# Four key stacks instead of three in a one-core cross-attention kernel

## What is computed

```python
q = (query @ Wq.T + bq).reshape(B, Sq, H, Hd).transpose(0, 2, 1, 3)      # H = 16 heads of Hd = 16
k = (key @ Wk.T + bk).reshape(B, Skv, H, Hd).transpose(0, 2, 1, 3)       # Skv = 375
v = (value @ Wv.T + bv).reshape(B, Skv, H, Hd).transpose(0, 2, 1, 3)
scores = jnp.einsum('bhqd,bhkd->bhqk', q * SCALE, k)
attn = jax.nn.softmax(scores, axis=-1)
out = jnp.einsum('bhqk,bhkd->bhqd', attn, v)
```

## Time and profile before

| | us |
|---|---|
| median of 3 executions | 563.15 (563.07 to 571.28) |
| the profiled execution, its own time | 567.81 |
| its span, first to last instruction | 566.1 |
| TensorE busy (68% of the span) | 384.2 |
| VectorE busy (68%) | 386.0 |
| ScalarE busy (47%) | 264.0 |
| GpSimd busy (16%) | 88.6 |

### The profile page before, as it was taken

The page is one execution under the profiler, slowest core; times in us unless marked ns, Lnnn a source line. Parts: engine busy times, 40 slices in busy tenths (PEclk is TensorE's granted clock), DMA queues, the critical chain, the costliest instruction groups (busy, mean ns, idle before and its releaser), DMA issues.

```text
span 566.1 us, 9319 instructions
## 1 busy us (share of the span) xinstructions
PE 384.2 (68%) x3004; PEld 256.1 (45%) x3004; DVE 386.0 (68%) x1614; ACT 264.0 (47%) x672; POOL 88.6 (16%) x274
## 2 busy tenths in 40 slices
PE   2899789912339699886898778898999701803006
PEld 2558576601127455563576566676545300203003
DVE  7644999989983768897776666672354477185773
ACT  3853534622221566345465555777453353243440
POOL 6793000000006064540240000000000000000000
PEclk9998699955557899889779998999999955855556
DMA  9800002368202598441675875500894000000002
GB/s 279 234 1 2 0 2 96 123 131 155 68 1 81 117 127 150 141 112 30 113 146 84 164 150 83 84 2 2 326 392 136 0 1 1 1 1 2 1 0 65
DMA packets 38533, 50.95 MB, mean 90 GB/s; under 512 B 5957, under 2 KB 35030, under 8 KB 37334
## 3 DMA queue, kind: packets, MB, share of 16 engines
q1 hardware_dynamic: 38486, 50.37, 37.3%
HBM read 40.28 MB, written 9.97 MB: 89 GB/s over the span
## 4 chain that ended last, share of the span: by engine, by line
PE 40%; DVE 34%; ACT 11%; issue 5%; DMA 5%; POOL 4%; SPq 1%; DVEq 0%; POOLq 0%; ACTq 0%
PE ps L2202 8%; DMA ks<-key_parts 5%; DVE PR L1080 5%; ACT below L1794 4%; PE ps L2036 4%; PE ps L2141 3%; PE ps L2166 3%; PE ps L2152 3%; DVE R L1014 2%; PE ps L1981 2%; DVE below L1417 2%; DVE prod L1076 2%; PE ps L1897 2%; PE ps L2326 2%; DVE PR L1078 2%
## 5 line engine op out<-in xcount | busy, mean ns | idle before, releaser
L1294 DVE TENSOR_REDUCE negm<-ps 112x1 f32<-112x375 f32 x128 | 64.1, 542 | 31.0 <-PE ps L2141 30.6
L1762 ACT ACTIVATE E<-ps 125x448 f32<-125x448 f32 x96 | 49.2, 546 | 30.0 <-PE ps L2152 28.3
L2141 PE MATMUL ps<-ks,qs 96*112 96x375 bf16 x128 | 45.0, 365 | 10.9 <-DMA ks<-key_parts 7.4
L2152 PE MATMUL ps<-qs,ks 99*125 99x112 bf16 x384 | 39.8, 230 | 5.2 <-ACT E L1762 3.4
L2152 PEld LDWEIGHTS ps<-qs,ks 99*125 99x125 bf16 x384 | 35.6, 145 | 13.2 <-ACT E L1762 9.8
L1282 DVE TENSOR_REDUCE acts<-gel 128x4 f32<-128x448 f32 x32 | 19.8, 620 | 30.9 <-ACT gel L1726 30.9
L2293 PE MATMUL ps<-cnt,same 128*128 128x7 bf16 (+1 forms) x22 | 3.6, 166 | 47.1 <-ACT below L1794 43.6
L2166 PE MATMUL ps<-E,v 125*32 125x112 f32 x768 | 32.3, 279 | 0.1
L811 POOL CAST kp<-kx 128x750 bf16<-128x750 f32 x8 | 6.5, 814 | 160.8 <-ACT path L1640 122.3
L1726 ACT ACTIVATE gel<-ps 128x448 f32<-128x448 f32 x32 | 17.3, 544 | 29.3 <-PE ps L2202 29.3
L1080 DVE TENSOR_TENSOR_SCAN PR<-UU,PR,prod 128x94 bf16<-128x94 bf16 x63 | 26.1, 414 | 2.2
(11 more groups left out here) (378 smaller groups left out, 1020.1 us busy)
## 6 DMA issues: line engine op xcount, KB each, us to landing
ks<-key_parts SPq DMA_DIRECT2D x48, 187.5 KB, 6.8
piwT<-fn_process_input_weights SPq DMA_DIRECT2D x4, 2048.0 KB, 16.6
key_parts<-kp SPq DMA_DIRECT2D x48, 93.8 KB
ctx_again<-in_ctx SPq DMA_DIRECT2D x7, 512.0 KB
keys<-kx SPq DMA_DIRECT2D x16, 187.5 KB, 2.2
kx<-keys SPq DMA_DIRECT2D x8, 375.0 KB, 5.9
ctxP<-in_ctx SPq DMA_DIRECT2D x8, 256.0 KB, 6.0
patT<-in_L_ffn_input_patterns SPq DMA_DIRECT2D x1, 2048.0 KB, 17.3
```

What stands on the lines that cost most here:

```text
L1294: drain(dve.tensor_reduce(negm[:, n:n + 1], bank(nm)[0:S, 0:SC], AX.X, ALU.max, negate=True), nm)
L1762: drain(fn(E[:, (KCH * f + c) % 6, :], bank(nm)[0:KC, 0:4 * S], ACT.Exp), nm)
L2141: fill(mm(bank(nm)[0:S, 0:SC], qs[0:SR, n, S * (u // 4):S * (u // 4) + S], ks[0:SR, u // 4 % 3, n, :], start=True, stop=True), nm)
L2152: ins = mm(bank(nm)[0:KC, S * i:S * i + S], ks[0:SR + 3, f // 4 % 3, n, KC * c:KC * c + KC], qs[0:SR + 3, n, S * (f // 4):S * (f // 4) + S ...
```

## The change

There is a fourth place for a key stack, `ks_last`, for the batches with b % 4 = 3. It lies at `queries_at`, over all of `qx32` and the first 4,832 bytes of `qp`, so it can be filled once the far queries have been written to DRAM. Its three rows of ones get a DMA of their own (`ones_last`), and TensorE waits for that once, at u = 12. SyncE now waits for the stores of both tiles of the far queries, issues the ones and stack 3, and then the twelve loads of the far queries. Stacks 4 to 7 are issued when the products of step 4b - 13 are done, four steps earlier than before. The patterns are issued behind stack 7.

```diff
@@ -385,6 +385,13 @@
         qp = rt.take("qp", [128, 2, 3, TOK], BF16)
+        ks_last = Region(queries_at).take("ks_last", [128, NH, SC], BF16)
+        assert queries_at + 2 * NH * SC <= rt.at
+
+        def stack(b):
+
+            return ks_last[:, :, :] if b % 4 == 3 else ks[:, b % 4, :, :]
+
         negm = rt.take("negm", [S, NH])
...
-        stack_loaded = [sem(f"stack_loaded{i}") for i in range(3)]
+        stack_loaded = [sem(f"stack_loaded{i}") for i in range(4)]
...
                 sp.wait_ge(parts_stored[b % 2], 96 * (b // 2 + 1))
                 for j, part in enumerate(K_PARTS):
-                    sp.dma_start(ks[HD * j:HD * j + HD, b % 3, :, :], key_parts[b, part]).then_inc(stack_loaded[b % 3], 16)
+                    sp.dma_start(stack(b)[HD * j:HD * j + HD], key_parts[b, part]).then_inc(stack_loaded[b % 4], 16)
...
             for half in range(2):
                 for t in range(2):
                     store_queries(half, t)
+                if half == 1:
+
+                    for t in range(2):
+                        sp.wait_ge(queries_stored[1][t], 48)
+                    sp.dma_start(stack(3)[SR:SR + 3], onesb[0:3, :].unsqueeze(1).broadcast_to([3, NH, SC])
+                                 ).then_inc(loaded["ones_last"], 16)
+                    load_stack(3)
                 for t in range(2):
                     load_queries(half, t)
-            for b in range(3, B):
-                wait_filled(sp, ("scoreT", 4 * b - 9, KCH - 1))
+            for b in range(4, B):
+                wait_filled(sp, ("scoreT", 4 * b - 13, KCH - 1))
                 load_stack(b)
-                if b == 4:
-                    sp.wait_ge(x_ready, 2 * B)
-                    sp.dma_start(patT[:, :, :], pat_in.rearrange("(h p) n -> p h n", p=128)).then_inc(loaded["pat"], 16)
+            sp.wait_ge(x_ready, 2 * B)
+            sp.dma_start(patT[:, :, :], pat_in.rearrange("(h p) n -> p h n", p=128)).then_inc(loaded["pat"], 16)
             wait_filled(sp, ("pv", B - 1))
...
                     if u % 4 == 0:
-                        pe.wait_ge(stack_loaded[u // 4 % 3], 16 * len(K_PARTS) * (u // 12 + 1))
+                        pe.wait_ge(stack_loaded[u // 4 % 4], 16 * len(K_PARTS) * (u // 16 + 1))
+                    if u == 12:
+                        pe.wait_ge(loaded["ones_last"], 16)
```

More of the change, by code:

```diff
@@ L491, in bankb @@
             return ps[plan[name].banks[0]][:, :].bitcast(BF16)
-        names = ("x",) + tuple(f"ctx{b}" for b in range(B)) + ("again", "ones_k", "attnW", "ffnW", "small", "biasT", "pat", "oiw",
+        names = ("x",) + tuple(f"ctx{b}" for b in range(B)) + ("again", "ones_k", "ones_last", "attnW", "ffnW", "small", "biasT", "pat", "oiw",
                  "opat", "pval", "piw")
@@ L632, in _ @@
             for b in range(3):
-                sp.dma_start(ks[SR:SR + 3, b, :, :], onesb[0:3, :].unsqueeze(1).broadcast_to([3, NH, SC])
+                sp.dma_start(stack(b)[SR:SR + 3], onesb[0:3, :].unsqueeze(1).broadcast_to([3, NH, SC])
                              ).then_inc(loaded["ones_k"], 16)
@@ L2140, in scores_for_maximum @@
                 n = 4 * (u % 4) + i
-                fill(mm(bank(nm)[0:S, 0:SC], qs[0:SR, n, S * (u // 4):S * (u // 4) + S], ks[0:SR, u // 4 % 3, n, :],
+                fill(mm(bank(nm)[0:S, 0:SC], qs[0:SR, n, S * (u // 4):S * (u // 4) + S], stack(u // 4)[0:SR, n, :],
                         start=True, stop=True), nm)
@@ L2152, in scores_less_maximum @@
                     ins = mm(bank(nm)[0:KC, S * i:S * i + S],
-                             ks[0:SR + 3, f // 4 % 3, n, KC * c:KC * c + KC],
+                             stack(f // 4)[0:SR + 3, n, KC * c:KC * c + KC],
                              qs[0:SR + 3, n, S * (f // 4):S * (f // 4) + S],
```

## The result

Over 20 runs each, the median is 560.09 us (554.89 to 565.44) against 566.14 us before (562.48 to 571.28); the ratio is 0.9887, with a 95% interval of 0.986 to 0.9914. The chip has a slower state in some executions, and all ratios here leave those out, so they differ a little from the ratio of the medians. The change gains about 6 us where 11.8 were forecast, and 560.09 lies outside the range. The profiled execution took 561.36 us against 567.81.

A forecast was written before the change was run, and what follows sets the result against it. The prediction took TensorE's waits for late key stacks, and the low clock behind them, to bound the loop. 13.3 us saved less a 1.5 us wait gave 11.8, so 563.15 would become 551.4 us, range 547.5 to 558.

The forecast's parts named there:

- the four pauses: TensorE's waits for a key stack at steps 7, 11, 15 and 19, together 10.07 us, to be removed.
- the list: Savings by loop step: 2.98 us at step 7, 1.02 at 8, 2.70 at 11, 3.73 at 15, 0.73 at 16, 2.16 at 19.
- the 13.3 us: Sum of the savings in the loop: 10.1 us of pauses and 3.2 us of low clock behind them.
- the 4.00 us that steps 7 and 8 were to give: Early in the loop: step 7 gives back 2.98 us of pause, step 8 gives back 1.02 us of low clock.
- the part on what is late next: Steps f % 4 = 3: VectorE and ScalarE charged nothing; if wrong, 0.6 to 1.5 us at each of four steps.
- the part on SyncE's queue: Load queue: the added wait for stores delays later loads; only step 11 waits, about 1.5 us, bounds 0 and 4.
- the wait of 1.5 us at step 11: Step 11: stack 4 lands at 318.6, asked for at 317.0; 1.5 us taken off the gain, bounds 0 and 4.
- Rival 2: Load queue fuller: step 11 waits 4 to 6 us, step 7 perhaps 1; gain 7 to 9, time 555; chance 0.12.
- Rival 3: Steps f % 4 = 3: VectorE's split or ScalarE's exponential waits up to 1.5 us each; gain 5.8, time 557.4; chance 0.09.
- Rival 1: Loop: low clock does not go with the pauses, 3.2 us not gained; gain 8.6, time 554.6; chance 0.17.
- Rival 4: Load queue: stack 3 lands no sooner or every load stretches; gain 0 to 3 us, time 562; chance 0.05.
- rival 5: Loop without pauses is denser and the clock falls for long stretches; slower, time up to 571; chance 0.04.

The follow-up runs named there:

- the kernel with four in flight: Changed kernel with stack 3 loaded early into the patterns' room, stack 7 over the query tiles, at most four DMAs issued but not landed; 549.11 us, ratio 0.9718.
- queries held: Changed kernel with the far queries held until step 4's score products are done and the patterns until stack 7 has landed; ratio 0.9871.
- four in flight: Changed kernel with at most four DMAs of stack 3, far queries and stack 4 not yet landed, patterns held until stack 7 has landed; ratio 0.9845.

## Why the prediction was wrong

**Right: what the four pauses and their clock cost.** Steps 11, 15, 16 and 19 took 6.07 + 7.10 + 3.34 + 5.53 = 22.04 us before and take 3.48 + 3.49 + 2.61 + 3.48 = 13.06 after. That is 8.98 us gained of the 9.32 that the list puts on them before its wait is taken off; the step with a stack takes 3.48, not 3.37. That the clean loop could give the 13.3 us is shown by the kernel with four in flight, whose loop is 14.1 us shorter than that of before (109.34 - 95.20), 12.8 of it in the six steps of the list.

**Wrong: the 4.00 us that steps 7 and 8 were to give, and nothing charged for TensorE's own instructions.** This is the step that failed. The part on what is late next charges nothing for VectorE and ScalarE, which held to 0.1 us a step, and the part on SyncE's queue looks at the landing of data; TensorE's own instructions, which come over the same DMA engines, stand in neither. Steps 7 and 8 were to give 4.00 us and lost 2.68 (9.82 + 2.84 against 6.35 + 3.63): 6.7 us of the miss, of which 4.14 is the stop and the rest mostly the lower clock over 6.8 us behind it. Steps 20 to 23 were to stay and took 16.47 instead of 15.70: 0.8 more, since the patterns behind stack 7 held back a block. The sentence "The patterns are issued near 334 instead of 315, and asked for at step 32" asked only when they land, not what stands behind them. With them held, that loss is gone (2.62 us for step 20).

**Hidden: the wait of 1.5 us at step 11.** It was 0, but for a bad reason: the stop at step 7 made TensorE come to step 11 late. The last DMA of stack 4 landed at 317.50 in the changed kernel. Without the stop TensorE would have asked for it near 315.9 (302.38, steps of 3.48, 2.62, 3.17 and 2.81, and 1.46 of work ahead of the product), so by this estimate a wait of 1.6 us would have been there: the prediction had it right, in mechanism and size. Its times for the queue were near too: stack 3 issued at 290.1 and landed near 301.5 by it, 288.15 and 299.75 in the trace; stack 4 landed at 318.6 by it. Where the stop was taken away a wait for stack 4 of 2.87 us (queries held) or 4.10 us (four in flight) did show, though in those kernels the stack is issued later.

**The sum again.** 11.8 - 6.7 - 0.8 + 1.4 (step 11 at 3.48 instead of 4.87) comes to 5.7, and the loop became 5.64 us shorter. The span became 6.4 shorter: the loop also starts 1.1 us earlier (281.70 against 282.78), and 0.3 is lost behind it.

**The rivals.** Rival 2 had the queue too full and step 7 among its places, but data as the victim. Rival 3 had the size, 5.8, and the wrong place: neither VectorE nor ScalarE is named for a wait in those steps. Rival 1 took the low clock to be loose from the pauses; in the changed kernel it follows the stops again, at 305.9 and 353.7. Rival 4 is out, since the stacks did come earlier, and so is rival 5: the densest loop, that of the kernel with four in flight, ran at 1.00. None of the five named the stop.

**The base.** The forecast started from 563.15, 3 us below the median of the twenty runs. From median to median the gain is 6.05 us, from profiled execution to profiled execution 6.45, about half the forecast both times; against 563.15 the measured 560.09 is only 3.1 us less.

## What to carry to other kernels

The wait that a deeper prefetch hides was gained in full here only when the queue stayed shallow: with the DMAs issued early and without a limit, TensorE's instruction packets came late. Give early loads a limit of issued but not landed DMAs, put what nobody needs soon behind a landing, and look for a stop ended by "issue" inside a run of instructions that has all its inputs; such stops stand multiples of 256 instructions apart here, and move to other work when the instruction count ahead of them changes, and a measured gain can move with them. Where a transfer can start before the crowded stretch, move it there first.

## What the runs showed of the hardware

- TensorE's instructions come in packets of 16,384 bytes, one for about 256 instructions. With the DMA engines full of data, one came 7.8 us after my estimate of when it was due, 8.5 us after the block end. A packet that TensorE was waiting for was followed by the next matmul 1.8 us after its end (305.49 to 307.30) or 1.4 (351.05 to 352.42).
- The delay looks like waiting for what SyncE had issued when the block was due, near 295.4: the far queries of tile 0, issued by 294.34, had all landed at 304.26, those of tile 1, issued by 297.34, at 309.20, and the packet started at 303.90. The Trainium skill, "DMA: Bandwidth & Descriptors", section on queues, rings and completion order, has each engine change in turn between the queues it has work for, packet by packet. By that a block would wait for a packet of SyncE's queue at each turn; the 7.8 us look like more than that, which is my reading and not shown. The trace shows only when the packet starts, not when it was asked for or where it stood, so which part of the path holds it is open. No run here tells it.
- From step 7 to step 20, block ends fall into steps 7, 10, 12, 15, 18 and 20 (with 64 more matmuls the ends at 3261 and 3517 fall into steps 8 and 11), and no such stop came elsewhere. Which of them a kernel shows is explained only in kind: a block must be due in a backlog. I did not count the block ends beforehand, and forecast the step to no better than three.
- With a limit of three in flight SyncE took 12.06 us to issue twelve query loads and with four 10.64, against 5.78 without a limit; the limit has a price where the data are needed soon.
